# Counting a chunk's edges per block for the second layer: one-hot columns summed by TensorE in place of a VectorE reduction

## The reference

```python
edge_index = jnp.stack([src, dst])
h = jnp.maximum(_layernorm(x), 0.0)
x = x + layer0(h, node_vec1, edge_attr_16, edge_attr_4, src, dst)      # gathers at src, segment mean over dst
h = jnp.maximum(_layernorm(x), 0.0)
x = x + layer1(h, edge_attr_3, edge_attr_64, edge_index)
# layer1:  src, dst = edge_index;  xs, xv = s[dst], v[dst]             # gathers at dst
#          tp  = products of xs, xv, w(edge_feature), direction(edge_attr)
#          agg = segment_sum(tp, src, num_segments=N) / 32             # sums over src
```

## Time and profile before

| | us |
|---|---|
| median of 3 runs | 9411.08 |
| lowest and highest | 9408.69, 9419.04 |
| span of the profiled execution | 9425.4 |
| POOL busy in the span | 6782.0 (72%) |
| DVE busy in the span | 7175.1 (76%) |
| PE busy in the span | 6599.8 (70%) |

### The profile page before, as it was taken

How to read it: one execution, slowest core, us unless ns; L and a number is a source line. 1 busy time by engine, 2 the same in 40 slices (tenths; PEclk the granted TensorE clock), 3 DMA queues, 4 the chain that set the end, 5 groups by cost and what they waited for, 6 DMA issues and landing times. The chain is left out here.

```text
span 9425.4 us, 173139 instructions
## 1 busy us (share of the span) xinstructions
PE 6599.8 (70%) x31166; PEld 4418.9 (47%) x31166; DVE 7175.1 (76%) x21240; ACT 4951.0 (53%) x16490; POOL 6782.0 (72%) x6877
## 2 busy tenths in 40 slices
PE   5566565654655565555555556678799999999999
PEld 3333333332222222222222222356588888888888
DVE  7666666665777676767777778977699999999995
ACT  3444444443444444444444445644477777777774
POOL 5777777777777777777777776456677777777770
PEclk7565555657888888888888888989899999999999
DMA  3222222225666666666666666545556666666667
GB/s 105 93 91 93 92 92 92 92 90 165 212 215 212 212 211 213 212 212 212 212 213 214 212 213 205 182 146 171 155 165 167 167 169 168 167 168 169 170 167 229
DMA packets 1189742, 1589.17 MB, mean 169 GB/s; under 512 B 452520, under 2 KB 967336, under 8 KB 1189544
## 3 DMA queue, kind: packets, MB, share of 16 engines
q1 hardware_dynamic: 789976, 836.56, 29.0%
q0 software_dynamic: 328704, 651.74, 24.2%
q10 hardware_dynamic: 70992, 100.14, 3.0%
HBM read 999.62 MB, written 1050.39 MB: 217 GB/s over the span
## 5 line engine op out<-in xcount | busy, mean ns | idle before, releaser
L1656 PE MATMUL pair<-prod_m,hot_m 128*128 128x160 f32 x14848 | 2245.1, 304 | 164.3 <-DVE prod_m L1862 128.1
L1543 POOL DMA_INDIRECT feat_m<-feat_tab,rows_m x1856 | 1830.9, 986 | 579.0 <-issue 441.9
L1656 PEld LDWEIGHTS pair<-prod_m,hot_m 128*128 128x128 f32 x14848 | 2043.6, 190 | 365.9 <-issue 361.3
L1677 ACT ACTIVATE hot_m<-hot_m,rows_m 128x128 f32<-128x128 f32 x5568 | 1728.5, 389 | 700.7 <-DVE hot_m L1845 694.8
L1554 POOL DMA_INDIRECT fetched_m<-feat_tab,index_m x1664 | 1673.2, 1006 | 518.5 <-issue 501.2
L663 POOL DMA_INDIRECT sorted_rows<-rows_e,place_e x1664 | 1611.6, 969 | 539.5 <-issue 503.9
L1689 ACT ACTIVATE prod_m<-part_m,rows_m 128x64 f32<-128x64 f32 x5568 | 1432.3, 337 | 1018.6 <-DVE part_m L1882 864.9
L1571 POOL DMA_INDIRECT sorted_rows<-later_m,place_m x1248 | 1243.9, 997 | 523.8 <-issue 376.4
L1637 PE MATMUL bank<-prod_m,hot_m 128*128 128x449 f32 x2476 | 1111.8, 572 | 575.6 <-DVE prod_m L1902 320.9
L1862 DVE TENSOR_TENSOR prod_m<-rows_m,feat_m 128x192 f32<-128x192 f32 (+2 forms) x4640 | 1282.7, 308 | 0.0
L488 PE MATMUL pair<-fc,hT_m 64*128 64x224 f32 x2496 | 405.5, 454 | 963.8 <-ACT later_m L1732 952.2
(11 more groups left out here) (264 smaller groups left out, 10303.2 us busy)
## 6 DMA issues: line engine op xcount, KB each, us to landing
agg_tab<-acc_m ACTq DMA_DIRECT2D x928, 320.0 KB
rows_m<-sorted_rows SPq DMA_DIRECT2D x928, 229.0 KB
agg_tab<-acc_m ACTq DMA_DIRECT2D x928, 224.5 KB
rows_m<-sorted_rows SPq DMA_DIRECT2D x928, 197.0 KB
feat_m<-feat_sorted SPq DMA_DIRECT2D x928, 160.0 KB
feat_sorted<-fetched_m SPq DMA_DIRECT2D x208, 640.0 KB, 5.3
turned_m<-in_turned ACTq DMA_DIRECT2D x159, 256.0 KB
agg_s<-agg_tab SPq DMA_DIRECT2D x98, 320.0 KB
```

What stands on the lines that cost most here:

```text
L1543: pool.indirect_dma_start(out=feat[s % RING][:, k, :], out_offset=None, in_=g.feat_tab[l.n], in_offset=bass.IndirectOffsetOnAxis(ap=rows[s ...
L1656: mm = pe.matmul(dst, hot[s % l.hot_bufs][:, k, q, :], rhs, start=(k == 0 and q < 2), stop=(k == ST_TILES - 1), skip_group_check=True)
L1677: ins = act.activation(hot[s % l.hot_bufs][:, k, 1 + q, :], hot[s % l.hot_bufs][:, k, 0, :], ACT.Copy, scale=rows[s % HELD][:, k, l.sh_at ...
```

## The change

Stages 2 and 3 no longer run `bin_count`. PE reads the one-hot itself: `columns_up` issues eight matmuls of 128 x 100, one per column, where `count_up` issued one. PE waits for `hot_made` in place of `hot_ready`. As PE now reads the one-hot also for the upper sum of the next chunk, the one-hot of the chunk after waits for `summed` (`bin_seen`). Stage 1 keeps `bin_count` and `count_up`.

```diff
+def bin_seen(dve, r, g, c, s, free):
+    if free is not None:
+        dve.wait_ge(r.summed, free)
+    bin_one_hot(dve, r, g, c, s, free)
+
+def columns_up(pe, r, s, which):
+    for k in range(CHUNK_TILES):
+        mm = pe.matmul(r.bank[:, 0:NBIN], which[:, :], r.hot[s][:, k, :], start=False, stop=True, skip_group_check=True)
+    return mm
...
                     if known >= 1:
                         pe.wait_ge(r.prod_ready, c)
-                        count_up(pe, r, 1 - h, g.upper_bf).then_inc(r.summed, 1)
-                    pe.wait_ge(r.hot_ready, c + 1)
-                    count_up(pe, r, h, g.lower_bf).then_inc(r.rank_ready, 1)
+                        columns_up(pe, r, 1 - h, g.upper_bf).then_inc(r.summed, 1)
+                    pe.wait_ge(r.hot_made, c + 1)
+                    columns_up(pe, r, h, g.lower_bf).then_inc(r.rank_ready, 1)
...
-                    bin_hot(nc, dve, r, g, c + 1, 1 - h, c if known >= 1 else None)
+                    bin_seen(dve, r, g, c + 1, 1 - h, c if known >= 1 else None)
...
                 w = window(step, it, s, 4)
...
-                    bin_one_hot(dve, r, g, c + 1, 1 - h, c if known >= 1 else None)
-                w = window(step, it, s, 5)
-                if w is not None:
-                    c, h, n, known = w
-                    bin_count(nc, dve, r, c + 1, 1 - h, c if known >= 1 else None)
+                    bin_seen(dve, r, g, c + 1, 1 - h, c if known >= 1 else None)
```

More of the change, by code:

```diff
@@ L1289, in _ @@
         def _(dve):
-            bin_hot(nc, dve, r, g, 0, 0, None)
+            bin_one_hot(dve, r, g, 0, 0, None)
             for s in range(DEEP):
@@ L1665, in _ @@
                 pe.wait_ge(r.prod_ready, NCHUNK0)
-                count_up(pe, r, (NCHUNK0 - 1) % 2, g.upper_bf).then_inc(r.summed, 1)
+                columns_up(pe, r, (NCHUNK0 - 1) % 2, g.upper_bf).then_inc(r.summed, 1)
         @block.scalar
```

## The result

The changed kernel takes 9313.06 us (median of 4 runs, 9293.21 to 9317.12), the kernel before 9412.45 beside it. The ratio is 0.989 (95% interval 0.9877 to 0.9903), faster by 1.1%; I had forecast 0.6%. The median lies at the low edge of my range (9312); the ratio on the old median gives 9308, just outside.

What follows compares the result with a forecast made beforehand. POOL was taken to bound stage 2 to about 5797 us, DVE its rest, and no full engine stage 3. Savings of 25 + 14 + 16 = 55 us took 9411 to 9356 us, range 9312 to 9402.

Steps and rivals of the forecast that it cites:

- DVE's last part of stage 2: Stage 2 from 5814 to 6146 us, where DVE is full: 18 counts of 1.41 us go, saving 25.4 us.
- Price of the matmuls: PE, stages 2 and 3: 14 more matmuls a chunk at 0.05 us, 0.7 us in all, hidden in stage 2.
- Rival D: Matmuls don't overlap, 2.9 us a chunk; stage 2 hides them, stage 3 pays: 9450 us, chance 4%.
- POOL's stretch: Stage 2, 2300 to 5797 us: 22 fewer prolonged POOL calls save 14 us; bounds 124 us saved to 112 us lost.
- rival C: Slower: DVE's shifted queue meets the wrong part of POOL's rhythm in nearly every chunk, 9482 us, chance 6%.
- the 13 calls: Of 78 counts between 2300 and 4340 us, 13 begin some 0.65 us after a POOL call that is then prolonged.
- the term of 16 us: Stage 3: 0.37 us a chunk, 19 us over 52 chunks, taken at 82% for the lower clock, saves 16 us.
- rival B: More than the sum: PE rests less in stage 3, clock stays up, or POOL is hit more rarely; 9309 or 9330, 18%.
- the chain through the DMA: Stage 3, from `x_sb` through the DMA to PE's next product: 11.33 us, not growing with the 14 matmuls.
- the first chain: Stage 3, from PE's product to DVE's `x_sb`: 11.04 us, falling to 10.31 without the count.
- the bound of 47 us: Stage 3's largest gain: the mean gap's excess over one chunk's, 12.1 - 11.2 = 0.9 us, over 52 chunks.
- Rival A: Only stage 2's last part gains; prolonged calls move elsewhere and stage 3 stays on its DMA chain: 9386 us, 17%.

Runs made afterwards that it cites:

- dead reduction: Changed kernel with the whole reduction run again on DVE, result unread: in stage 3 9436.01 us (1.0022), in stage 2 at its old place 9346.87 us (0.9924).
- early count: Kernel before, with stage 2's reduction straight behind the one-hot instead of a step later: 9417.23 us (0.9997).
- half a reduction: Changed kernel with a reduction over half of the bins at the old place in stage 2, result unread: 9347.27 us (0.9925).
- half of it: Changed kernel with a reduction over half of the bins on DVE in stage 3, result unread: 9328.38 us (0.9901).
- moved reduction: Kernel before, with stage 3's reduction moved to the end of DVE's odd step and PE's two matmuls a chunk kept: 9356.22 us (0.9936).
- rest filled: Kernel before, with eight matmuls, their result overwritten, run in PE's rest ahead of `hidden` in stage 3: 9380.6 us (0.9958).
- stage-3-only kernel: Kernel before with the change in stage 3 alone, stage 2 keeping its reduction: 9349.09 us (0.9932).

## Why the prediction fell short

The direction and the places of all three terms were right; the size was not, and nearly all of the miss is stage 3.

*DVE's last part of stage 2: right.* 25.4 us forecast, 26.3 measured, and the dead reduction gives it back.

*Price of the matmuls: right.* 0.05 us each forecast, 0.046 measured, hidden in stage 2. The 81 ns that the Trainium skill (TensorE: Matmul & The Clock Gate, "Back-to-back issue gap") gives at 128 columns would have put the two groups of eight an estimated 0.65 us apart. With 100 columns they start 0.37 us apart here. Rival D, which needed more than 0.1 us a matmul (its 0.12 is a little high: 1.43 / 14 = 0.10), is out.

*POOL's stretch: sign and bounds right, reason wrong.* I wrote that the calls beside the count become short because the operation which follows now prolongs none. Of the calls of 1.2 us or more in the stretch, counted in the merged timelines of POOL and DVE (135 before, 99 after), the first DVE operation that starts in them, the super-tile's products left aside, is now in 17 the super-tile's one-hot and in 37 the accumulation (L1933), which had 11; the rank's product fell from 41 to 10 and its sum from 47 to 31. In the kernel with the early count no prolonged call is beside the reduction, and the last fetch is no earlier.

That grouping names what follows, as the prediction did. What the prolonged calls have in common are the products left aside, each a TENSOR_TENSOR of two operands in SBUF (`rows_m`, `feat_m` and `part_m` are buffers there). The call of the earlier trace rows that starts at 2347.62 has these two in it, ahead of the count:

```profile
2347.83 0.28 DVE L1855 TENSOR_TENSOR prod_m<-rows_m,feat_m 128x128 f32<-128x128 f32 x1
2348.04 0.35 DVE L1902 TENSOR_TENSOR prod_m<-part_m,rows_m 128x192 f32<-128x192 f32 x1
```

A call of the changed kernel, with the short one-hot of the next super-tile behind the products:

```profile
2470.12 1.59 POOL L1568 DMA_INDIRECT fetched_m<-feat_tab,index_m  x1 [0.30 <-issue]
2470.34 0.28 DVE L1865 TENSOR_TENSOR prod_m<-rows_m,feat_m 128x128 f32<-128x128 f32 x1
2470.54 0.35 DVE L1912 TENSOR_TENSOR prod_m<-part_m,rows_m 128x192 f32<-128x192 f32 x1
2470.81 0.47 DVE L1855 SCALAR_TENSOR_TENSOR hot_m<-pair,base_node,rows_m 128x256 f32<-128x256 f32 x1
```

Both calls end 1.37 us after the 128x128 product starts. That product starts 0.10 to 0.31 us into 123 of the 135 prolonged calls and 62 of the 99, and all but one of these end 1.36 to 1.46 us after its start, whether count, rank sum, rank product or one-hot follows. In 11 and 37 others it is L1883 (L1893 after), the product ahead of the accumulation, and the call ends 1.16 to 1.19 us after that one starts. The converse holds for before: all 115 calls in which the 128x128 product starts 0.15 to 0.30 us in are prolonged, while of the other calls in which the rank's sum or the count starts, 84 and 93, only 5 and 1 are. So the prolonged calls go with the products and not with the count. The prediction saw none with the one-hot behind the products because before the change no call of that alignment had it there; now 17 do.

The time of the prolonged calls over 0.95 us each fell from 81 to 53 us, which is the 28. They are what the new alignment of DVE's queue with POOL's calls happened to give; half a reduction's shift gave the opposite, rival C's mechanism at a smaller price. The rule that I weighed (the Trainium skill, SBUF — State Buffer, "SBUF: two separate sides") lets a `tensor_reduce` with one input hold up no call, and lets an operation with two SBUF inputs hold up a GpSimd operation that reads SBUF. The traces agree with both, and I was wrong to set the 13 calls against it. Why only a product in that part of a call prolongs it, while 1385 other calls of before have a product starting in them and stay short, is not shown by these runs, and none of them moves or removes the products alone.

*Stage 3: the term of 16 us that measured 62 (74 in the first pair).* Three steps of it failed. First, "a mean of 0.91 between half and full is 82% of the time at full, so 0.82 x 19": I took the clock of before as given for after. It rose to 0.99. PE's rests are what changed:

| stage 3 of | PE's rests in the stretch, us | longest, us | products of 1.6 us or more | clock |
|---|---|---|---|---|
| before | 97 of 569 | 2.96 | 21 of 94 | 0.91 |
| after | 35 of 495 | 1.58 | 0 of 95 | 0.99 |
| dead reduction | 108 of 634 | 2.92 | 32 of 95 | 0.87 |
| half of it | 75 of 549 | 2.38 | 8 of 95 | 0.97 |
| moved reduction | 64 of 507 | 2.01 | 8 of 96 | 0.97 |
| rest filled | 6 of 540 | 0.92 | 0 of 96 | 1.00 |

(Rests over 0.1 us between PE's rows and products by their length, from the timelines.) In the earlier trace rows one product follows 0.50 us of rest and takes 1.34; the chunk behind it, on which the prediction did not draw, has these lines in before:

```profile
6343.91 2.05 PE L1130 MATMUL bank<-turned_c,fc 128*128 128x512 f32 x2 [2.13 <-DMA turned_c<-in_turned]
6345.75 1.77 PE L1178 MATMUL pair<-w_out,aggT_c 128*128 128x161 f32 x8
```

After 2.13 us of rest `hidden` takes 2.05 in place of 1.12. I had named this as rival B ("PE rests less in stage 3, so the clock stays up") at 18%; 9330 and 9309 were its times. That the clock gave 29 us is shown by the filled rest, where nothing else changed for the better; that the sixteen matmuls are not what keeps it up, by the dead and the moved reduction.

Second, the chain through the DMA. Its 11.33 us went to the product's start at 6337.61, and that row says 0.50 us of waiting for `x_sb`: a wait for the first chain, counted into the second. Without it the second is 10.83 and the mean of the two 10.57, not 10.82.

Third, the bound of 47 us. It was the excess of the mean gap over a chunk at full clock, which is the clock's part alone; the shorter chain comes on top. And I did not look for what would bind next: POOL's eight sends at 0.96 + 0.30 us are 10.1 us a chunk, so no more than (12.1 - 10.1) x 47 = 94 us was to be had in the 47 gaps of the earlier trace rows, and at 10.37 the stage has stopped there.

Rival A fell with the stage-3-only kernel.

## What to carry to other kernels

Take a chain apart row by row and leave out of it every wait for the other chain; then look for the engine whose issue rate binds next, which gives the floor. Where PE's granted clock in a stage is below full, price an edit at both clocks and ask whether it shortens PE's rests: here the clock gave as much as the chain itself, a reduction moved into DVE's own rest gave nearly as much as its removal, and with the long chain kept, more matmuls in the chain made the kernel slower than before, while more in PE's rest made it faster. Before an operation is blamed for a prolonged call, list everything that starts in the call, and look for calls that have the operation and are not prolonged. A gain on a saturated POOL that comes from where another engine's operations happen to fall is not the edit's own: shift one operation and see whether it stays.

## What was not expected of the hardware

POOL's indirect DMA calls answer to alignment and not to load: with 0.75 us of DVE work added a chunk the fetches went from 984 to 1016 ns and the sends from 1001 to 984, with 1.5 us added to 1005 and 993. What the prolonged calls share is a product of two SBUF operands that starts early in them, and their end follows it at a fixed distance, 1.37 us in both calls shown above.

One rest of PE does not settle its clock: behind 1.55 us of rest `hidden` took 1.12 us in the earlier trace rows, while in the kernel with the moved reduction it took 1.72 behind 1.59, and the next product 2.35:

```profile
6402.78 1.72 PE L1130 MATMUL bank<-turned_c,fc 128*128 128x512 f32 x2 [1.59 <-DMA turned_c<-in_turned]
6404.30 2.35 PE L1178 MATMUL pair<-w_out,aggT_c 128*128 128x161 f32 x8
```

The unchanged stage 3 differs by 21 us between executions, and its span goes with the granted clock: 601.9 us at 0.91, 591.1 and 591.6 at 0.92, 581.0 at 0.94. Why the clock falls more often in one execution than in another is open.
